# A conditioned three-way MLP with an adapter on one Trainium2 core: a new order of the two-layer steps on all engines

## What is computed

```python
nr  = gelu(x @ w1_nr + b1_nr) @ w2_nr + b2_nr                     # c == 0: two layers
tsr = gelu(x @ w1_tsr + b1_tsr) @ w2_tsr + b2_tsr                 # c == 1: two layers
sr  = gelu(gelu(x @ w1_sr + b1_sr) @ w2_sr + b2_sr) @ w3_sr + b3_sr  # c == 2: three layers, 512 wide inside
y   = layernorm(x + {0: nr, 1: tsr, 2: sr}[c]) * gamma + beta
h   = gelu(y @ down_W.T + down_b)                                 # 64 wide
h   = h @ expert_W[d].T + expert_b[d] + domain_emb[d]
out = layernorm(h @ up_W.T + up_b + y) * ln_gamma + ln_beta
```

## Time and profile before

| | us |
|---|---|
| median of three runs | 275.27 (274.41 to 281.27) |
| the profiled execution | 270.76 |
| its span, first to last instruction | 269.0 |
| granted TensorE clock, mean share of full speed | 0.993 |
| TensorE matmul busy | 250.9 |
| VectorE busy | 204.7 |
| ScalarE busy | 193.0 |
| GpSimd busy | 149.1 |

### The profile page before, as it was taken

One profiled execution on the slowest core, in us unless ns is written; L12 is line 12 of the kernel. 1 busy time (PEld: TensorE's weight loads), 2 busy tenths in 40 slices (PEclk: granted clock), 3 DMA queues, 4 the chain that ended last, 5 costly groups with the idle time before them and its releaser, 6 DMA issues.

```text
span 269.0 us, 8352 instructions
## 1 busy us (share of the span) xinstructions
PE 250.9 (93%) x2116; PEld 222.2 (83%) x2117; DVE 204.7 (76%) x724; ACT 193.0 (72%) x446; POOL 149.1 (55%) x168
## 2 busy tenths in 40 slices
PE   8998999999999998899999999999999999999670
PEld 7698998999999987788898888888898888888550
DVE  6769543474764764988889888888888888989784
ACT  3578479569669576687878788888878778887440
POOL 3134474473675573756656555556656555558463
PEclk9999999999999999999999999999999999999997
DMA  6372011012022122133242434233332434232133
GB/s 190 91 264 64 12 41 43 5 42 49 30 60 60 37 59 59 39 78 82 74 98 68 107 87 108 68 88 78 78 98 68 107 84 111 66 92 60 40 83 101
DMA packets 44098, 20.63 MB, mean 77 GB/s; under 512 B 37782, under 2 KB 42348, under 8 KB 44077
## 3 DMA queue, kind: packets, MB, share of 16 engines
q1 hardware_dynamic: 41385, 15.18, 23.0%
q0 software_dynamic: 1536, 4.20, 4.6%
q10 hardware_dynamic: 1156, 1.00, 1.3%
HBM read 11.69 MB, written 8.65 MB: 76 GB/s over the span
## 4 chain that ended last, share of the span: by engine, by line
PE 72%; issue 10%; DVE 8%; POOL 5%; DMA 2%; ACT 1%; DVEq 1%; POOLq 0%; ACTq 0%
PE ps_h L1058 19%; PE ps_z L1129 12%; PE ps_u L1181 9%; PE ps_z L1134 5%; PE ps_z L1093 5%; PE ps_t L1151 5%; PE ps_d L1194 4%; PE ps_u L1093 4%; POOL rs L484 2%; POOL h_lo L477 2%; PE ps_t L1232 2%; PE ps_t L1235 2%; PE ps_t L1233 2%; DVE n L717 1%; PE ps_u L1016 1%
## 5 line engine op out<-in xcount | busy, mean ns | idle before, releaser
L477 POOL TENSOR_TENSOR h_lo<-h,h_hi 128x256 fp32r<-128x256 f32 (+1 forms) x75 | 70.2, 936 | 75.9 <-ACT h L887 75.3
L484 POOL TENSOR_TENSOR rs<-ve,minus_half 128x4 f32<-128x4 f32 (+1 forms) x38 | 41.1, 1081 | 27.9 <-DVE ve L693 27.6
L894 ACT ACTIVATE zn<-ps_z,nm,rs 128x256 f32<-128x256 f32 x66 | 33.7, 562 | 28.9 <-DVE nm L697 28.9
L887 ACT ACTIVATE h_hi<-ps_h,per_feature_sb 128x256 fp32r<-128x256 f32 x84 | 38.8, 494 | 16.4 <-PE ps_h L1058 15.3
L681 DVE BATCH_NORM_STATS2 st<-ps_z 128x6 f32<-128x256 f32 x66 | 24.9, 418 | 31.9 <-PE ps_z L1134 31.9
L1129 PE MATMUL ps_z<-last_hi,h_hi 128*128 (+1 forms) x132 | 36.0, 305 | 3.3 <-issue 3.0
L913 ACT ACTIVATE yt<-ps_t,per_feature_sb 128x256 f32<-128x256 f32 x66 | 34.1, 574 | 6.5 <-PE ps_t L1151 6.4
L887 ACT ACTIVATE h<-ps_h,per_feature_sb 128x256 f32<-128x256 f32 x84 | 38.7, 497 | 0.0
L511 POOL DMA_INDIRECT out<-o,out_rows_now x32 | 34.2, 1069 | 8.0 <-issue 5.4
L1181 PE MATMUL ps_u<-tables,stack 65*64 x132 | 35.6, 392 | 0.0
L1181 PE MATMUL ps_u<-second_table,stack 65*64 65x256 f32 x132 | 35.6, 392 | 0.0
(11 more groups left out here) (148 smaller groups left out, 629.4 us busy)
## 6 DMA issues: line engine op xcount, KB each, us to landing
x<-in_x_feat SPq DMA_DIRECT2D x130, 64.0 KB, 2.2
out<-o SPq DMA_DIRECT2D x65, 64.0 KB, 2.0
last_sb<-in_last_w SPq DMA_DIRECT2D x1, 768.0 KB, 4.7
w_sr_sb<-in_w_sr SPq DMA_DIRECT2D x1, 512.0 KB, 3.6
w_sr_sb<-in_w_sr ACTq DMA_DIRECT2D x1, 512.0 KB, 4.5
w_two_sb<-in_w_two SPq DMA_DIRECT2D x1, 512.0 KB, 5.4
out<-o,out_rows_now POOLq DMA_INDIRECT x32, 2.6
per_unit_sb<-in_per_unit SPq DMA_DIRECT2D x1, 268.1 KB
```

What stands on the lines that cost most here:

```text
L477: pool.tensor_tensor(dst, full, high.bitcast(F32), ALU.subtract).then_inc(ready, 1)
L484: pool.tensor_tensor(RS[p][:, norms, :], VE[p][:, norms, :], half_of_two[:, norms, :], ALU.pow).then_inc(rstd, 1)
L887: ins = act.activation(dst[:, m, :], src[m], ACT.Gelu, bias=COL[:, bass.ds(col + m, 1)])
L894: ins = act.activation(ZN[:, t, :], ZP[p][:, t, :], ACT.Identity, bias=NM[p][:, t:t + 1], scale=RS[p][:, 0, t:t + 1])
```

## The change

No arithmetic is changed. On each engine the same instructions stand in another order:

- TensorE: in `finish_other` the transposes of slot `g-1` stand between the two halves of the first layer of slot `g+1`, and the register load of the table numbers stands ahead of the first half. SR steps have their old order.
- VectorE, in every step of head and main, SR or two-layer: statistics, moments and variance of slot `g` come directly one after another, then centring, then the copies of the second tables (now for slot `g-1`), nm, o, and only then x_lo, the statistics and moments of `ps_u`, and the bias. In the last step but one the copies of slot `g-1` are added.
- GpSimd, in two-layer steps: rs, h_lo, indirect store, h_lo. SR steps have their old order.
- ScalarE: x_hi ahead of yt where the first layer of a two-layer slot is followed by yt; zn ahead of stack, in all steps.

```diff
@@ gpsimd
                     low(h1l[:, 2:4, :], h1[:, 2:4, :], h1h[:, 2:4, :], h1_full, h1_lo, g + 1)
+                    if where != LAST1:
+                        store(g, i, p, where)
                 with pool.Else():
+                    powers(g, i, p, where)
                     for slot in on_slot(g, -1, where):
                         low(h2l[:, 0, :], h2[:, 0, :], h2h[:, 0, :], h0_full, h0_lo, g + 1)
-                    powers(g, i, p, where)
+                    if where != LAST1:
+                        store(g, i, p, where)
                     for slot in on_slot(g, -1, where):
                         low(h2l[:, 1, :], h2[:, 1, :], h2h[:, 1, :], h1_full, h1_lo, g + 1)
-                if where != LAST1:
-                    store(g, i, p, where)
@@ vector
                 for slot in on_slot(g, 0, where):
                     first_stats(slot, p)
+                    first_moments(slot, p)
+                variances(p, BOTH)
                 for slot in on_slot(g, 3, where):
                     center(slot, q, p)
+                for slot in on_slot(g, 1, where):
+                    copy_second_tables(slot, q)
                 for slot in on_slot(g, 0, where):
-                    first_moments(slot, p)
-                variances(p, BOTH)
+                    minus_mean(slot, p, where)
+                for slot in on_slot(g, 3, where):
+                    finish(slot, i - 2 if p == 0 else i - 1, q, where)
                 for slot in on_slot(g, -2, where):
                     input_low(slot, p)
                 for slot in on_slot(g, 2, where):
@@
-                for slot in on_slot(g, 0, where):
-                    minus_mean(slot, p, where)
-                for slot in on_slot(g, 3, where):
-                    finish(slot, i - 2 if p == 0 else i - 1, q, where)
                 for slot in on_slot(g, -2, where):
                     dve.wait_ge(x_lo, slot + 1)
                     add_bias(slot, p)
-                for slot in on_slot(g, 0, where):
-                    copy_second_tables(slot, p)
@@ scalar
                         with act.Else():
                             first_of_two(False)
+                            next_input(g, i, p, where)
                             for slot in on_slot(g, 1, where):
                                 residual_norm(slot, q, where)
-                next_input(g, i, p, where)
@@
+                for slot in on_slot(g, 0, where):
+                    normalise(slot, p, where)
                 for slot in on_slot(g, 1, where):
                     adapter_gelu(slot, q)
-                for slot in on_slot(g, 0, where):
-                    normalise(slot, p, where)
@@ tensor, finish_other
-                start_two(g, 1 - p, where)
-                adapter(g, p, where)
+                at = [tables_of(slot) for slot in on_slot(g, 2, where)]
+
+                def transposes_of_z():
+                    for slot in on_slot(g, 1, where):
+                        transposes(slot, where)
+
+                start_two(g, 1 - p, where, transposes_of_z)
+                adapter(g, p, where, at)
```

48 lines of the change are left out of this document (25 added, 23 removed).

## The result

The changed kernel takes 309.37 us (median of four runs, 305.67 to 310.1), the kernel before 274.84 in the same comparison: a ratio of 1.129 (95% interval 1.122 to 1.135), 34.5 us slower. The forecast was 295.6, with a range from 285 to 303. The sign was right and the size too small by 14 us, outside the range.

What follows compares the result with a forecast made beforehand. TensorE's order of work was taken to set the time, its waits paid in full. SR stage 13.8, change of kind 1.8, two-layer steps 3.8 and tail 0.9 sum to 20.3, on 275.3: 295.6 us, range 285 to 303.

Steps and rivals of the forecast that it cites:

- SR steps, the wait: Three-layer (SR) steps: TensorE waits for the later x_lo, 1.98 us in each of four steps, 13.8 us over seven.
- rival (a): SR steps: nm is not held behind rs, so they lose 6 us instead of 13.8; 287.8 us, chance 0.10.
- Rival (d): SR steps: TensorE's 2 us waits drop its clock to 1.2 GHz, tens of us more; chance 0.02.
- Behind the change of kind: First two-layer step: TensorE waits for the second h_lo until 5.3 us behind the statistics' start, 1.1 us later than before.
- the mean of 1.05: GpSimd in two-layer steps: the indirect store ahead of the second h_lo was taken as 1.05 us.
- hidden, and only just: Two-layer steps: VectorE's chain, with nm held for one h_lo, takes 6.1 to 6.2 us, under TensorE's 6.23.
- the forecast's alternation: Two-layer steps: two kinds alternate on TensorE, (6.93 + 5.54) / 2 = 6.23 us a step against 6.06.
- the 3.8: Two-layer steps: TensorE's register load ahead of the first layer, behind the late second h_lo, costs 3.8 us over 22 steps.
- rival (c): VectorE: table copies are held through rs and the following h_lo, in SR and two-layer steps; 316 us, chance 0.05.
- The edits costed at nothing: Two-layer steps: the other edits, such as earlier zn and x_hi ahead of yt within ScalarE's slack, cost 0 us.
- the 1.1 us: First two-layer step: GpSimd's store ahead of the second h_lo makes TensorE start 1.1 us later.
- The end: Last step but one: later first h_lo (0.73 us) and one more VectorE copy (0.47), taken as 0.9 us.

Runs made afterwards that it cites:

- e3: Changed kernel with six unread matmuls of ones added ahead of TensorE's wait for x_lo in each three-layer step: 302.94 us.
- e4: Changed kernel with nm made by two instructions of one tensor input each, instead of one with two: 301.89 us.
- e8: Changed kernel with e4's nm and GpSimd's old order in the two-layer steps: 301.18 us.
- e7: Kernel before with VectorE's whole new order alone: 309.35 us.
- e10: Kernel before with GpSimd's new order alone: 303.42 us.
- e6: Changed kernel with VectorE's whole old order put back: 303.13 us.
- e12: Changed kernel with GpSimd's h_lo in two-layer steps made for one column only, the rest set to zero: 301.43 us.
- e5: Changed kernel with e4's nm and TensorE's register load put back behind the first layer: 310.06 us.
- e9: Kernel before with TensorE's new order alone: 276.37 us, where the kernel before took 272.15.
- e13: Kernel before with ScalarE's new order alone: 279.32 us, where the kernel before took 274.53.

## Why the prediction was right and wrong

**In sum.** Of the 19.0 us that the forecast lacks between the two spans (39.3 for 20.3), 5.4 lie in the SR steps, 3.4 behind the change of kind, 5.8 in the steady two-layer steps and 4.4 at the end.

**SR steps, the wait: right.** x_lo was forecast to end at Z + 5.25 and TensorE to start at Z + 5.30. It ended at 67.45 and TensorE started at 67.50, with Z = 62.28: Z + 5.17 and Z + 5.22. The sum of the waits is 13.3 us by e3, 13.8 forecast; that it came so near is in part luck, since the first two were put 0.4 too high each. nm was held, 1.10 us, as the earlier trace rows had shown. The side sum of 6 us for an nm that isn't held was added up wrong (1.1 in four steps, 1.4 in two and 0.1 in one are 7.3, so rival (a) stood for 289.1 us), and its premise was wrong too: e4 and e8 show that o is held in its place, and e8's seven steps at full clock are still 12.2 us longer than before. That rival could not have come true as I priced it.

**SR steps, the clock: the step that failed.** Rival (d), given 0.02, came true beside the forecast: 6.0 us in the SR steps. Its argument rested on one row, a wait of 2.01 us that kept the clock. One wait at full clock says that a fall isn't certain, not that it is unlikely for seven waits in a row; the changed kernel has both kinds. The forecast's own sum put the clock at nothing. The rival was also priced wrongly, as all or nothing ("tens of us"), where each fall cost 1.5 us.

**Behind the change of kind: 4.9 us for 1.4.** The wait that was forecast is there, for the second h_lo behind the store: TensorE's low products start at 133.28, which is Z + 6.65, where Z + 5.3 was forecast and the kernel before had Z + 4.2. It isn't the only cause: e7, without GpSimd's new order, loses 2.0 us here, and e8, which takes that order back from e4, gains 1.2. (e10 loses 4.7, but all its two-layer steps are 1.4 us longer.) Two terms were off:

```profile
130.04 2.42 POOL L511 DMA_INDIRECT out<-o,out_rows_now  x1 [0.17 <-issue]
132.49 0.74 POOL L477 TENSOR_TENSOR h_lo<-h,h_hi 128x256 fp32r<-128x256 f32 x1
```

The store took 2.42 us where I had put the mean of 1.05, and TensorE, which waited 3.37 us for that h_lo, went on at half clock from 132.15 to 138.97. What made this one store so long is open: in e6 and e10 the first store behind the change of kind took 1.21 us, and TensorE waited 3.1 us all the same, with VectorE's old list and its later variance.

**Two-layer steps: 9.1 us for 3.3.** I had TensorE as the bound at 6.23 us, with steps of two kinds in alternation, and VectorE "hidden, and only just" at 6.1 to 6.2 with nm held. In the changed kernel's first nine steady steps VectorE is the bound instead: they take 6.49 us each and it never waits for z. The term that failed there is the price of the hold. I had let one instruction meet one h_lo, and taken nm's hold as part of the 6.2; there are two h_lo a step, has the duration of each, nm and the copies are held for 0.53 us in sum, and e7, VectorE's list alone, has 6.56 with TensorE and GpSimd as before.

From slot 20 on the forecast's alternation is there, 6.9 and 6.3 us in turn, 6.60 in the mean, and VectorE waits for z in every other step:

```profile
227.91 0.76 DVE L683 BATCH_NORM_STATS2 st<-ps_z 128x6 f32<-128x256 f32 x2 [0.47 <-PE ps_z L1135]
232.55 0.75 POOL L477 TENSOR_TENSOR h_lo<-h,h_hi 128x256 fp32r<-128x256 f32 x1
233.35 0.74 PE L1135 MATMUL ps_z<-last_hi,h_lo 128*128 x4
234.65 0.38 PE L1059 MATMUL ps_h<-x_hi,w_two_hi 128*128 128x256 f32 x1 [0.56 <-issue]
240.46 0.64 PE L1135 MATMUL ps_z<-last_hi,h_lo 128*128 x4
```

From Z = 227.91 it is 5.44 us to the low products behind the second h_lo (5.25 forecast), 1.30 to the first layer (1.0), 5.81 to the next low products (5.54) and 0.67 to the next such Z at 241.13 (0.68): 13.2 us for two steps, where the forecast's terms give 12.5. So there its mechanism was right and three of its terms too small. With two paths this close, taking one away brings little: e4 lightens VectorE's and e12 does so fully, e5 takes the register load out of the other, and none has steps under 6.44 us. The register load, on which the 3.8 rested, costs 0.09 us a step by itself (e9). How the 9.1 us divide between the paths stays open.

The Trainium skill (SBUF — State Buffer, "Who interferes with whom") has a VectorE instruction with two inputs in SBUF, and copies too, fully blocked while a GpSimd instruction that reads SBUF holds the pair of ports they share. nm, o, the copies and x_lo all showed it against h_lo here. Against rs the copies did not: rival (c) had them held already from rs on, and the pair at 64.34 took its 0.48 us with rs running from 63.72 to 64.86. Only h_lo held them.

**The edits costed at nothing.** x_hi ahead of yt and zn ahead of stack cost 5 us by themselves (e13), and GpSimd's order 31 (e10), where the forecast had given it only the register load's delay and the 1.1 us. In the changed kernel GpSimd's order is worth 0.1 us a step (e8 against e4); ScalarE's wasn't taken back there, so its share isn't shown. That they came to so little in the sum was luck of the combination and no result of my argument, which had not looked at GpSimd's order with a late variance at all.

**The end: 5.4 us for 0.9.** All kernels with VectorE's old list take 29 to 31 us here, those with the new one 33 to 36, but for e12. In the changed kernel TensorE works at half clock from 289.16 to 295.99, where the page of the kernel before has a lower clock in its last slice only; that part was not foreseen. How much of the 5.4 us it is wasn't worked out.

None of the experiments beats the kernel before. Each engine's part of the change is slower than it alone, TensorE's and ScalarE's by 2%.

## What to carry to other kernels

When a low-priority instruction is moved behind a wait, price its consumer's new start, then ask what a repeated idle gap does to TensorE's clock: here a gap cost 2 us as a wait and, in four of seven cases in one kernel and none in another, 1.5 us more. Treat the time in which GpSimd's two-input work holds VectorE as an amount that lands on whichever instruction comes next, not as a property of one instruction that can be rewritten. And where an order is changed on several engines at once, look for the loops that run through three of them: the price of one edit alone says little about the whole (75 us as the sum of four, 35 together).

## What the runs showed of the hardware that was not expected

- Filling TensorE's gap with six matmuls that nobody needs made the kernel 6.4 us faster (309.37 to 302.94); 4.4 us of it lie in the SR steps, by the clock.
- A GpSimd instruction of four columns (rs, 1.14 us, both inputs in SBUF) did not hold the copies that started under it (0.48 us for two), where h_lo held copies, nm, o and x_lo.
- The stretches at half clock that follow waits of 1.7 to 2.4 us are not tied to the wait's length alone: in one kernel 1.76 us was followed by one and 2.41 was not. Yet at the last three SR waits, 1.8 to 1.9 us was followed by one in nine of nine cases over three kernels, and 1.6 to 1.7 us in none of twelve over four.
- A VectorE instruction on one column with one tensor input ran beside an h_lo without being held (0.33 us for two of them) where the same product with two tensor inputs took 1.10.
- The issue of the indirect store on GpSimd is not constant: 0.98 to 2.42 us within the changed kernel, with a median of 1.21.
